# Attention scores with keys on the partitions, and values beside 64 columns of ones, in a fused graph and attention network

## The reference

```python
q = (x @ wq).reshape(B, S, N_HEADS, D_K).transpose(0, 2, 1, 3)
k = (x @ wk)...; v = (x @ wv)...            # k and v repeated to 8 heads
scores = jnp.einsum('bhqd,bhkd->bhqk', q, k) / jnp.sqrt(jnp.float32(D_K))
attn = jax.nn.softmax(scores, axis=-1)
out = jnp.einsum('bhqk,bhkd->bhqd', attn, v)
out = out.transpose(0, 2, 1, 3).reshape(B, S, D_MODEL)
return out @ wo
```

## Time and profile before

| what | value |
|---|---|
| median of 3 runs | 1966.99 us |
| the profiled execution | 1966.68 us, span 1964.9 us |
| PE busy | 1617.7 us (82%) |
| VectorE busy | 806.2 us (41%) |
| ScalarE busy | 507.0 us (26%) |
| GpSimd busy | 391.3 us (20%) |
| chain that ended last, by engine | PE 57%, DMA 16%, VectorE 13%, ScalarE 6% |
| first PE product of the layer's projections (L1018) | at 711.83 us |
| first scores (L1033) | at 801.93 us |
| first product of `ffn_o` (L1068) | at 1167.41 us |

### The profile page before, as it was taken

How to read it: one execution, slowest core, us unless ns; L and a number is a source line. 1 busy time by engine, 2 the same in 40 slices (tenths; PEclk the granted TensorE clock), 3 DMA queues, 4 the chain that set the end, 5 groups by cost and what they waited for, 6 DMA issues and landing times.

```text
span 1964.9 us, 19619 instructions
## 1 busy us (share of the span) xinstructions
PE 1617.7 (82%) x7674; PEld 1101.6 (56%) x7674; DVE 806.2 (41%) x1517; ACT 507.0 (26%) x734; POOL 391.3 (20%) x248
## 2 busy tenths in 40 slices
PE   1999969799998759888888886899889651999895
PEld 1546644366556548677777763555766541655452
DVE  5021160699204642577777755250344324111100
ACT  1210011021201132577777741100223110101000
POOL 3100030200301120344444424100220002222112
PEclk9999989899998879899999998999999855999997
DMA  4000100100110011100000012000200452799993
GB/s 171 0 0 1 41 4 0 59 1 1 82 46 1 6 65 66 27 14 14 14 14 14 22 37 120 0 22 0 86 1 0 206 206 95 285 403 400 408 418 126
DMA packets 23236, 170.74 MB, mean 87 GB/s; under 512 B 4259, under 2 KB 4805, under 8 KB 16886
## 3 DMA queue, kind: packets, MB, share of 16 engines
q1 hardware_dynamic: 19568, 164.44, 21.2%
q0 software_dynamic: 3584, 5.12, 1.2%
HBM read 153.06 MB, written 16.49 MB: 86 GB/s over the span
## 4 chain that ended last, share of the span: by engine, by line
PE 57%; DMA 16%; DVE 13%; ACT 6%; issue 5%; POOL 2%; another core or an unknown queue 1%; SPq 0%; DVEq 0%; POOLq 0%; ACTq 0%
PE psum L839 16%; DMA out_x<-arena,idx 12%; PE psum L849 9%; PE psum L866 6%; PE psum L978 6%; PE psum L1063 5%; PE psum L858 4%; PE psum L1051 3%; DVE arena_r L1458 3%; PE psum L1033 3%; DMA xf_dram<-arena 2%; DVE neg_max L1437 2%; ACT arena_r L762 1%; DVE ln_st L1217 1%; DVE arena L1225 1%
## 5 line engine op out<-in xcount | busy, mean ns | idle before, releaser
L839 PE MATMUL psum<-arena 125*128 125x512 f32 (+3 forms) x864 | 308.0, 518 | 14.2 <-DMA arena<-in_w_in 11.4
L839 PEld LDWEIGHTS psum<-arena 125*128 125x128 f32 (+1 forms) x864 | 164.5, 191 | 157.1 <-issue 143.3
L866 PE MATMUL psum<-arena 128*125 128x512 f32 (+3 forms) x464 | 163.0, 510 | 20.6 <-DVE arena L1565 9.0
L542 POOL TENSOR_SCALAR arena<-arena,row_inv 125x1250 f32<-125x1250 f32 x40 | 138.5, 3462 | 192.3 <-DVE row_inv L1445 192.3
L1198 PE MATMUL psum<-arena 128*39 128x512 f32 (+1 forms) x704 | 159.2, 609 | 13.0 <-DMA arena<-in_w_down 10.2
L1051 PE MATMUL psum<-ident,arena 125*125 125x125 f32 x800 | 125.8, 283 | 49.7 <-DVE arena_r L1458 48.4
L1458 DVE TENSOR_TENSOR arena_r<-psum,arena_r 125x500 fp32r<-125x500 f32 x200 | 131.9, 673 | 42.2 <-ACT arena_r L762 29.2
L1051 PEld LDWEIGHTS psum<-ident,arena 125*125 125x125 f32 x800 | 102.8, 188 | 63.0 <-DVE arena_r L1458 58.2
L762 ACT ACTIVATE arena_r<-psum 125x500 fp32r<-125x500 f32 x200 | 114.5, 587 | 87.9 <-PE psum L1051 87.8
L866 PEld LDWEIGHTS psum<-arena 128*125 128x125 f32 (+2 forms) x464 | 81.2, 191 | 99.1 <-issue 71.0
L978 PE MATMUL psum<-arena 125*125 125x512 bf16 (+1 forms) x588 | 120.1, 358 | 13.0 <-DVE arena L1349 11.5
(11 more groups left out here) (283 smaller groups left out, 2019.1 us busy)
## 6 DMA issues: line engine op xcount, KB each, us to landing
arena<-in_w_down SPq DMA_DIRECT2D x32, 2816.0 KB, 22.6
arena<-in_w_up SPq DMA_DIRECT2D x32, 682.5 KB, 19.7
a_spill<-arena SPq DMA_DIRECT2D x1, 6103.5 KB
arena<-a_spill SPq DMA_DIRECT2D x1, 6103.5 KB
bc<-k_dram SPq DMA_DIRECT2D x16, 312.5 KB, 4.3
gw<-in_gw SPq DMA_DIRECT2D x2, 2048.0 KB, 10.7
arena<-in_wkqv SPq DMA_DIRECT2D x1, 3072.0 KB, 16.5
arena<-in_x SPq DMA_DIRECT2D x10, 250.0 KB
```

What stands on the lines that cost most here:

```text
L542: pool.tensor_scalar(PR[i], PR[i], row_inv[:, i:i + 1], None, ALU.mult).then_inc(p_even, 1)
L839: ins = pe.matmul(o[0:w, lo:hi], lhs(c, m), rhs(c)[:, lo:hi], start=c == 0, stop=c == k - 1)
L866: ins = pe.matmul(o[0:p, 0:w], lhs(c, t), rhs(c, t), start=c == 0, stop=c == k - 1)
```

## The change

Scores are made with the keys on the partitions. Their exponents can then be the moving operand of the product with the values as they stand, so the transposes, the two parts of the exponents and the scaling of rows by POOL and ACT are gone. The work of a head is now 30 steps: three rounds of 420 queries (they overlap by a few queries, 3 x 420 for 1250), each with 10 tiles of 125 keys.

- A step's scores (L1087, L1088 of the new file) are two fp32r products of 420 columns. The second has 65 rows: the low part of the keys and, as row 65, ones, against the high part of the queries and, as row 65, the negated maximum of each query (`QM`). So the maximum is subtracted by the product.
- The maximum is taken from scores of its own, which only need to be near: `max_scores` (L1058), three fp32r products per tile of 125 queries with queries on the partitions and `KHH` alone, into `max_bank`; the same DVE reduction as before (L1495). `turn_max` (L1071) turns ten columns of maxima into rows, and ACT copies them into row 65 of `QM` (L780).
- ACT takes the exponent of a step (L791) from a ring of three PSUM banks into one of 7 tiles `PT`.
- One plain fp32 product per step (L1098) multiplies `VA`, the values of a head beside 64 columns of ones, with `PT`. Its lower 64 rows are the sums, already on all 64 partitions. At a round's end DVE takes their reciprocal (L1504, 64x420) and multiplies (L1506) into `ATT`.
- `ffn_k` is now computed before `ffn_q`; the values' weights are split only after the keys have been stored, because their high part now lies where `KF` was. The maxima of head 0 are taken between the tiles of `ffn_v`. SP copies each head's `QS` high part into `QM`. The load of `woa` has moved to the start.

```diff
+QW, QH = 420, 210
+ROUNDS = [(0, QW), (416, 416 + QW), (N - QW, N)]
+STEPS = len(ROUNDS) * TILES
+BATCH = 3
+P_RING = 7
@@ sync
+                sp.wait_ge(q_hi, h + 1)
+                if h == 0:
+                    sp.wait_ge(rows_full, ROW["ffn_v"] + TILES)
+                if h:
+                    sp.wait_ge(ring_full, step_entry(STEPS * (h - 1)) + 1)
+                load("qm", QM[h % 2][0:DK].bitcast(F32), QS[64 * (h % 2):64 * (h % 2) + 64, h].bitcast(F32))
+                if h == 0:
+                    load_chosen("woa", WOA)
@@ gpsimd
-                pool.tensor_scalar(PR[i], PR[i], row_inv[:, i:i + 1], None, ALU.mult).then_inc(p_even, 1)
+            pool.wait_ge(cols_full, COL["ffn_q"] + 4)
+            pool.memset(VA[:, :, :, DK:2 * DK], 1.0).then_inc(v_ones, 1)
+            pool.wait_ge(rows_full, ROW["ffn_v"] + TILES)
+            pool.wait_ge(v_ones, 1)
+            for i in range(2):
+                pool.memset(KLO[i][DK:DK + 1].bitcast(F32), 1.0).then_inc(k_ones, 1)
+            for h in range(HEADS):
+                split_keys(h)
@@ scalar
+            act.wait_ge(loads["wv"], 16)
+            act.wait_ge(k_stored, 16)
+            act.activation(WV_PARTS[0], WV, ACT.Copy).then_inc(proj_hi, 1)
...
+            for s in range(HEADS * STEPS):
+                h, at = divmod(s, STEPS)
+                act.wait_ge(ring_full, step_entry(s) + 1)
+                if s >= P_RING:
+                    act.wait_ge(av_step, s - P_RING + 1)
+                act.activation(PT[s % P_RING], ring(step_entry(s))[:, 0:QW], ACT.Exp).then_inc(ring_done, 1)
+                if at == 14 and h + 2 < HEADS:
+                    key_highs(h + 2)
+                if at == STEPS - 1 and h + 1 < HEADS:
+                    max_row(h + 1)
@@ tensor
             for t in range(TILES):
                 split_row(ROW["ffn_v"] + t, t, XLT_PARTS, WV_PARTS)
+                if t < 8:
+                    max_scores(0, t)
+                if 7 <= t < 9:
+                    max_scores(0, t + 1)
...
+            turn_max(0)
+            pe.wait_ge(k_ones, 2)
+            pe.wait_ge(v_ones, 1)
+            max_scores(1, 0)
+            batches = HEADS * STEPS // BATCH
+            for j in range(batches):
+                h, b = divmod(j, STEPS // BATCH)
+                score_batch(j)
+                if h + 1 < HEADS and b < 9:
+                    max_scores(h + 1, b + 1)
+                if b:
+                    weigh_batch(j - 1)
+                if b == 9:
+                    if h + 1 < HEADS:
+                        turn_max(h + 1)
+                    if h + 2 < HEADS:
+                        max_scores(h + 2, 0)
+                    weigh_batch(j)
@@ vector
+            def normalise_heads(rnd):
+                dve.wait_ge(av_step, TILES * (rnd + 1))
+                dve.reciprocal(sum_inv[:], av_bank[rnd % 2][DK:2 * DK]).then_inc(sum_inverted, 1)
+                dve.wait_ge(sum_inverted, rnd + 1)
+                dve.tensor_tensor(ATT[own, h // 2, q0:q1], av_bank[rnd % 2][0:DK], sum_inv[:], ALU.mult).then_inc(att_ready, 1)
```

More of the change, by code:

```diff
@@ L745, in scale_odd @@
[L745 to L770 removed]
+                act.activation(VA[:, t, :, 0:DK], row_psum(ROW["ffn_v"] + t)[0:TOK, :].rearrange("p (h d) -> p h d", d=DK),
+                               ACT.Copy).then_inc(rows_free, 1)
@@ new lines, in weigh_batch @@
+            def weigh_batch(j):
+                for s in range(BATCH * j, BATCH * j + BATCH):
+                    h, at = divmod(s, STEPS)
+                    rnd, t = divmod(s, TILES)
+                    if t == 0 and rnd >= 2:
+                        pe.wait_ge(att_ready, rnd - 1)
+                    pe.wait_ge(ring_done, step_entry(s) + 1)
+                    pe.matmul(av_bank[rnd % 2], VA[:, t, h], PT[s % P_RING], start=t == 0,
+                              stop=t == TILES - 1).then_inc(av_step, 1)
@@ new lines, in _ @@
+            for t in range(TILES):
+                bound(0, t)
+            bound(1, 0)
+            for s in range(HEADS * STEPS):
+                h, at = divmod(s, STEPS)
+                rnd, t = divmod(s, TILES)
+                if at % BATCH == BATCH - 1:
+                    if h + 1 < HEADS and at < STEPS - 1:
+                        bound(h + 1, at // BATCH + 1)
+                    if h + 2 < HEADS and at == STEPS - 1:
+                        bound(h + 2, 0)
+                if t == 7 and rnd:
+                    normalise_heads(rnd - 1)
```

269 lines of the change are left out of this document (112 added, 157 removed), and 2 rows, old and new, of the table loads.

## The result

The changed kernel takes **1943.02 us** (median, 1938.90 to 1944.34 in four runs) where the kernel before takes 1966.99 (1966.48 to 1969.98 in four): a ratio of 0.987, 95% interval [0.9854, 0.9889]. The profiled execution took 1938.9 us, 27.8 less than the profiled one of before, with a span of 1937.1. The prediction was 1939.3, between 1930 and 1956.

What follows compares the result with a forecast made beforehand. PE was nearest to being the bound, missing 52.9 us, of which 48.4 waited for VectorE's L1458. 819.8 + 310.3 + 3.9 + 2.0 + 3.7 = 1139.7 for `ffn_o` against 1167.4, 27.7 less: 1939.3 us, range 1930 to 1956.

Steps and rivals of the forecast that it cites:

- rival 4: Value and score products on PE: weight loads exposed by each product's own wait, 0.19 us each, 91 us, 2030; chance 0.06.
- 310.3 us: PE's work from head 0's first step on: scores 93.6, maxima 40.7, value products 169.0, turning the maxima 7.0.
- VectorE's cover: Two reductions with a round's normalisation between take 8.4 us, bank wanted at 8.9: hidden, with 0.5 us to spare.
- rival 1: VectorE's 64x420 reciprocal from PSUM is slower, 8.2 ns a column, 3.43 us: 4 us more, 1943; chance 0.10.
- (a): Before the steps: ScalarE waits for the keys' store before splitting the values' weights and draining the first query tile; 2.1 us.
- (b): Before the steps: the first maximum needs all query tiles drained; cost 1.7 us.
- (c): Head 0's ten maxima between the value tiles, 5.8 us; two follow each other directly, one reduction exposed, 1.7.
- (d): Serial chain of memsets, low keys, load and high part before head 1's first maximum, which starts at 819.8 us.
- (e): Lower clock behind the wait before head 1's first maximum: 2.0 us in the sum.
- 2: Rival: each satisfied semaphore wait costs PE about 0.02 us, some 560 products, 11 us, 1950; chance 0.08.
- 3: Rival: the lower clock lasts longer and returns after the wait at the end, 3 and 1.5 us more, 1944; chance 0.10.
- 5: Rival: PE's steps wait for ScalarE after all; at 0.35 us a batch nothing is left, 1967; chance 0.04.

Runs made afterwards that it cites:

- b1_half: The kernel before, with VectorE's low part of the exponents (L1458) formed for 250 of 500 columns; 1939.82 us.
- m1_nomax: The changed kernel without the maxima of heads 1 to 7 and their reductions (69 tiles); 1897.89 us.
- f2_recip: The changed kernel with each round's reciprocal on VectorE done twice, the first result unused; 1992.51 us.
- f3_waits: The changed kernel with the ring's and the exponents' waits once per batch of three steps instead of before each product; 1943.58 us.
- e1_tail: The changed kernel with the first six tiles of `ffn_o` waiting only for round 23 of 24; 1940.09 us.
- after: The changed kernel itself, as first measured and profiled; 1943.02 us.
- a_again: The changed kernel run again, unaltered, beside the combined kernels; 1942.8 us.
- best: The changed kernel with the tail, order and weights edits, head 0's maxima one tile later and the low-key ones written later; 1929.80 us.
- f1_fp32r: The changed kernel with the value product in fp32r, values and exponents rounded without a low part; 1876.31 us.

## Why the prediction was right, point by point

The mechanism held, and not only the number: the old heads waited for L1458 (b1_half), the new ones are bound by TensorE's products (m1_nomax), and the stretch was the sum of them.

**PE's paces** hold to 1%: 0.195 for an fp32r product of 420 columns and 0.352 for a record of fp32 were worked out by slope and by proportion; the loads start 0.19 to 0.20 and 0.35 apart, and six records stand in the chain with 2.12 us, 0.353 each. The batch: 3.86 forecast, 3.85 measured; the head 39 to 40, measured 39.8 (860.29 to 900.10). The loads also refute rival 4: none of those with a wait of their own is late. The one term of the 310.3 us that was off is the small products for turning the maxima: 0.10 each was taken, ten take 0.60 us, so 4.2 instead of 7.0. It was the value without a row, and the slope's 0.07 was the nearer end.

**VectorE's cover** was the tightest number and it held. Reciprocal 2.78 forecast, 2.784 measured, from two rows of 1 and of 80 columns; tensor product 0.59 and 0.59; reduction 1.449 and 1.458; cover 0.5 forecast, 0.54 by the timeline (888.38 to 888.92), 0.6 to 0.8 by f2_recip. How often an excess would be paid was wrong: 24 times by the prediction, 13 times and at the end in f2_recip. Nothing hung on it, since there was no excess. The first, short batch of a head cost 0.40 us instead of 0.55, seven times. The 2.784 us decide for 6.25 ns a column and against rival 1's 8.2, which would be 3.43 us.

**Before the steps** each new wait was found and sized: (a) 2.1 forecast, 2.0 measured; (b) 1.7 and 1.5; (c) 1.7 and 1.5; end of the value stage 808.3 and 808.2; (d) head 1's first maximum at 819.8 and 820.04, where errors in the terms cancel: GpSimd's memsets were 1.13 instead of 1.3 each, but head 1's two loads of keys took 5.3 us from the first issue at 813.39 to ScalarE's start at 818.66, with 4.3 forecast; (e), the 2.0 in the sum for the lower clock behind that wait: about 1.7. No run shows the 2.0: the earlier trace rows have a granted clock of 0.50 for 3.0 us and of 0.55 for 9.8. In the changed kernel the clock fell during the wait, with a mean of 1.00 from 808 to 812, 0.69 to 816 and 0.50 to 820; it was still 0.50 up to 823.5 and 1.00 from 824.0.

**The end.** 3.7 forecast, 3.54 measured. `ffn_o` was forecast for 1139.7 and began at 1137.33: 2.8 us from the small products, 1.1 from the heads' first batches and small change the other way.

**The rivals.** 1 is real as a mechanism and absent at this price (f2_recip); its sum at the double price came out by luck. 2 and 4 are refuted (f3_waits, and the loads above). The column times that 2 takes off, 0.104 and 0.213 us, stand in no row of the prediction; in the trace of before, nine bf16 products of L978, 3750 columns, take 1.58 us from the load at 428.52 to the one at 430.10, which by proportion gives 0.105 and 0.216 for 250 and 512 columns, an estimate. 3 came in a form of its own: the clock was low again, 0.56, for the first 3.7 us of `ffn_o`. 5 fell with the batch of 3.85.

**What the prediction did not see.** It let everything after `ffn_o` move along as a block, since `ffn_o` and the adjacency's load hang on one event. It does, but neither of these two is on the path: the landing of `w_in`, queued behind the adjacency, is, some 57 us after the heads' end, and `ffn_o` with its norms and transposes has 11 us of slack before it. The rows for that were in the trace of before, where the wait is 11.4 us. For this change the two readings give the same sum, since both hang on the heads' end; for the next edit they don't: e1_tail gains nothing by the one and 3.5 us by the other. The 2.3 us given back after `ffn_o` are 1.3 for a later landing of the load (57.6 from the first issue to `x_mid`, 56.3 before) and 1.0 in the rest, within what the last stage's traffic varies.

The median came 3.7 us above the forecast although the profiled execution, 1938.9, is within 0.1 us of the 1939.0 for its like. So the last step, that the profiled run stands as near to the median as before (0.3 us), failed: here it is 4.1 under it. The projections' clock, which alone made 3 us between the traces of after and a_again, is a candidate; it was not shown for these runs. What the layer does can be forecast closer than which of its runs a trace shows.

## What to carry to other kernels

Before trading many cheap products for fewer dear ones, add up the rhythm of each engine over one batch: the change won over the kernel before with as much work for TensorE as it had, because TensorE then has next to nothing to wait for (13.1 of 324.9 us without a product). The length of the dear fp32 form hides a 2.8 us reciprocal that the cheap form lays bare, though the cheap form is still the faster one. And a smaller edit may be worth as much: half of one instruction of VectorE was, in b1_half. Where several stages hang on one event, ask which wait ends last behind it, above all on a load queued behind a large one: moving a 6.1 MB load behind a 1 MB one was worth 15 us together with an earlier start of one stage, more than the 13 us of all edits of order in best. And check each microsecond that an edit frees against the next wait in the trace before counting it.

## What the runs showed of the hardware

- A 1 MB load issued behind a 6.1 MB one landed after 56.9 us; issued ahead of it, after 8.1.
- A weight load of 0.19 us is wholly hidden under products of 0.195 us, also where 128 and 65 rows take turns and every second product has its own semaphore wait; waits that are already satisfied cost nothing measurable (two of three taken away, in f3_waits: 362.1 us from values to heads' end, against 361.2).
- Waits of about 2 us in TensorE's stream can cost more than their length: in f2_recip 27 us more of them came with 23 us more busy time for the same products, at a mean granted clock of 0.93. They don't always: in f1_fp32r one wait of 2.22 us was followed by products at a granted clock of 1.00, and another of 2.23 us by products at 0.50. The trace does not say why.
- VectorE's reciprocal takes 0.159 us for 1 column, 0.653 for 80 and 2.784 for 420, thus 6.3 ns for each column behind the first. The longest reads PSUM and the two others SBUF.
- The same instructions can take 3 us more in the projections of one execution than in another (after and a_again, start to values 64.5 and 67.5 us), by the clock that is granted: 0.94 and 0.61 from 714 to 718 us.
